# Low-rank layers on transposed activations: SP asks for all four x tiles of a group before the adapters, and asks for the A and B halves of the adapters separately

## What is computed

```
# layer 1: 8 adapters of rank 16, all in one 128-row matrix; ids per sequence
x = x + x @ W1.T + bias1 + scale[id] * (x @ A1[id].T) @ B1[id].T
# layer 2: 32 adapters of rank 16, gathered per sequence
x = x + x @ W2.T + bias2 + 2 * (x @ A2[id]) @ B2[id]
```

## Time and profile before

| | |
|---|---|
| median of 3 runs | 2545.6 us (2545.35 to 2546.51) |
| profiled execution, its own time | 2544.21 us |
| its span | 2542.6 us |
| PE busy over the span | 2409.0 us (95%) |
| changed stage, 105 to 317 us: PE busy | 162.41 of 212 us |
| granted PE clock in that stage | 0.88 of full speed (0.976 over the whole span) |

### The profile page before, as it was taken

The page is one execution under the profiler, slowest core; times in us unless marked ns, Lnnn a source line. Parts: engine busy times, 40 slices in busy tenths (PEclk is TensorE's granted clock), DMA queues, the critical chain, the costliest instruction groups (busy, mean ns, idle before and its releaser), DMA issues. The chain is left out here.

```text
span 2542.6 us, 54643 instructions
## 1 busy us (share of the span) xinstructions
PE 2409.0 (95%) x16070; PEld 2195.2 (86%) x16071; DVE 1780.3 (70%) x3632; ACT 1602.2 (63%) x3311; POOL 599.9 (24%) x896
## 2 busy tenths in 40 slices
PE   6878799999999979999999999999999997699999
PEld 4656688888888869999999999999999997588887
DVE  5434334989998977888878878788788884544443
ACT  3223235877777778888888888888888884311111
POOL 1200012000000024444444444444544442000000
PEclk9889999999999989999999999999999999799999
DMA  6521132333333469888888898888888884766664
GB/s 221 174 64 55 61 140 88 103 100 113 99 100 99 133 192 302 291 295 297 303 281 304 285 294 303 282 300 293 292 301 281 299 276 161 273 206 213 210 213 148
DMA packets 373752, 536.83 MB, mean 211 GB/s; under 512 B 49314, under 2 KB 263010, under 8 KB 369826
## 3 DMA queue, kind: packets, MB, share of 16 engines
q1 hardware_dynamic: 301538, 311.62, 38.2%
q0 software_dynamic: 70016, 221.30, 25.6%
q10 hardware_dynamic: 2112, 2.89, 0.4%
HBM read 437.35 MB, written 98.30 MB: 211 GB/s over the span
## 5 line engine op out<-in xcount | busy, mean ns | idle before, releaser
L1669 PE MATMUL both_ps_o<-att_pt,att_v 128*128 128x128 f32 x4096 | 539.3, 275 | 0.0
L1367 ACT ACTIVATE att_prob<-att_prob,att_shift 128x544 f32<-128x544 f32 x512 | 384.4, 751 | 205.5 <-DVE att_shift L1387 195.8
L1669 PEld LDWEIGHTS both_ps_o<-att_pt,att_v 128*128 128x128 f32 x4096 | 504.0, 191 | 0.0
L1387 DVE CUSTOM_DVE_ANT_0 att_prob<-both_ps_s,att_mask 128x544 f32<-128x544 f32 x512 | 365.0, 713 | 0.0
L102 PE MATMUL both_ps_s<-att_k_hi,att_q_hi 128*128 128x272 f32 x1024 | 339.2, 331 | 4.8 <-DVE att_k_lo L1362 4.8
L1362 DVE TENSOR_TENSOR att_k_lo<-att_k_raw,att_k_hi 128x1024 fp32r<-128x1024 f32 (+1 forms) x320 | 338.6, 1058 | 1.9 <-ACT att_k_hi L1356 1.9
L1646 PE MATMUL both_ps_pt<-both_ident,att_prob 128*128 128x128 f32 x2048 | 309.2, 274 | 7.8 <-ACT att_prob L1367 6.2
L104 PE MATMUL both_ps_s<-att_k_hi,att_q_lo 128*128 128x272 f32 x1024 | 298.0, 291 | 0.0
L1545 ACT ACTIVATE att_pt<-both_ps_pt 128x512 f32<-128x512 f32 x512 | 294.3, 575 | 2.2 <-PE both_ps_s L1654 1.2
L103 PE MATMUL both_ps_s<-att_k_lo,att_q_hi 128*128 128x272 f32 x1024 | 295.3, 288 | 0.0
L1356 ACT ACTIVATE att_k_hi<-att_k_raw 128x1024 fp32r<-128x1024 f32 (+1 forms) x320 | 292.7, 915 | 0.0
(11 more groups left out here) (209 smaller groups left out, 5036.0 us busy)
## 6 DMA issues: line engine op xcount, KB each, us to landing
att_k_raw<-in_k_pages SPq DMA_DIRECT2D x1024, 128.0 KB, 4.8
q_t<-qkv_out_t SPq DMA_DIRECT2D x128, 256.0 KB, 2.3
att_q_raw<-q_t POOLq DMA_DIRECT2D x64, 512.0 KB, 7.5
o_t<-att_o POOLq DMA_DIRECT2D x64, 512.0 KB, 7.0
out_o<-o_t SPq DMA_DIRECT2D x32, 1024.0 KB, 6.0
out_inv<-inv_t SPq DMA_DIRECT2D x32, 1024.0 KB, 6.6
both_w_stage<-in_w_qkv SPq DMA_DIRECT2D x12, 1024.0 KB, 5.2
l_w_stage<-in_w SPq DMA_DIRECT2D x8, 1024.0 KB, 7.4
```

The costliest lines, as they stand in the source:

```text
L1367: act.activation(prob[:, b, :], prob[:, b, :], ACT.Exp, bias=shift[:, b:b + 1], scale=-1.0, accum_out=total[:, j // HK, j % HK:j % HK + 1] ...
L1387: dve.tensor_tensor_reduce(out=prob[:, b, :].rearrange("p (a n) -> p a n", a=2), in0=ps_s[:, j % 2, :, 0:HALF], in1=mask[:, j // HK, :].re ...
L1669: pe.matmul(out, v_sb[p][:, c, h * DH:(h + 1) * DH], pt_sb[:, j % OG, c, :], start=(c == 0), stop=False)
```

## The change

SP's program in `lora_layers` is written in another order. All four x tiles of a group are asked for together; input tiles rotate through all four `x_sb` buffers (so x14 and x15, whose buffers the results z0 to z3 use as well, wait for the stores of those). In `load_adapters` the 8 A's of a half are issued in a row, as soon as the same half of the A buffer has been split, then the 8 B's, as soon as the same half of the B buffer has been split. Two semaphores (`a_loaded`, `b_loaded`), each counting both halves, replace one per half. No arithmetic changes, nor do the orders of PE and DVE.

```diff
                 def load_x(t):
                     if t >= 4:
-                        sp.wait_ge(turned, TURN_OF["x", t - 4 if t < 6 else t - 2] + 1)
-                    sp.dma_start(x_sb[:, x_buf(t), :], x_in[rows(t), :]).then_inc(x_loaded[x_buf(t)], 16)
+                        sp.wait_ge(turned, TURN_OF["x", t - 4] + 1)
+                    if t >= NT - 2:
+                        sp.wait_ge(both.x_stored[t % 2], 16 * 2)
+                    sp.dma_start(x_sb[:, t % 4, :], x_in[rows(t), :]).then_inc(x_loaded[t % 4], 16)
...
                         if g:
-                            sp.wait_ge(ab_split, 4 * g)
+                            sp.wait_ge(ab_split, 4 * (g - 1) + h + 1)
                         elif h:
                             sp.wait_ge(weights_split, FIRST_OF[W2])
                         for s, a in enumerate(adapters):
                             sp.dma_start(a_in[:, h, s * KC * RANK:(s + 1) * KC * RANK], i["a2"][bass.ds(a, 1)])\
-                              .then_inc(ab_loaded[h], 16)
+                              .then_inc(a_loaded, 16)
+                        if g:
+                            sp.wait_ge(ab_split, 4 * (g - 1) + 2 + h + 1)
+                        for s, a in enumerate(adapters):
                             sp.dma_start(b_in[s * RANK:(s + 1) * RANK, h, :], i["b2"][bass.ds(a, 1)])\
-                              .then_inc(ab_loaded[h], 16)
+                              .then_inc(b_loaded, 16)
...
-                for t in range(TPG, TPG + 2):
+                for t in range(TPG, 2 * TPG):
                     load_x(t)
                 sp.dma_start(w_in[:, 1, :, :], i["w2"]).then_inc(weights_loaded[W2], 16)
                 sp.wait_ge(ids2_loaded, 16)
                 load_adapters(0)
-                for t in range(TPG + 2, TPG + 4):
+                for t in range(2 * TPG, 3 * TPG):
                     load_x(t)
                 sp.wait_ge(weights_split, FIRST_OF[B1])
                 sp.dma_start(w_in[:, 0, :, :], w_next).then_inc(kept.w_loaded[0], 16)
-                for g in range(1, LG):
-                    if g < LG - 1:
-                        for t in range(TPG * (g + 1), TPG * (g + 1) + 2):
-                            load_x(t)
-                    load_adapters(g)
-                    if g < LG - 1:
-                        for t in range(TPG * (g + 1) + 2, TPG * (g + 2)):
-                            load_x(t)
-                    for t in range(TPG * (g - 1), TPG * g):
-                        store(t)
+                load_adapters(1)
+                for t in range(3 * TPG, NT - 2):
+                    load_x(t)
+                for t in range(TPG):
+                    store(t)
+                for t in range(NT - 2, NT):
+                    load_x(t)
+                load_adapters(2)
+                for t in range(TPG, 2 * TPG):
+                    store(t)
+                load_adapters(3)
+                for t in range(2 * TPG, NT - TPG):
+                    store(t)
...
                 def a_hi_part(g):
+                    act.wait_ge(a_loaded, 16 * 2 * HS * (g + 1))
+                    if g:
+                        act.wait_ge(low_done, ROUND_OF[1, g - 1] + 1)
                     for h in range(2):
-                        act.wait_ge(ab_loaded[h], 16 * 2 * HS * (g + 1))
-                        if g:
-                            act.wait_ge(low_done, ROUND_OF[1, g - 1] + 1)
...
                 def b_hi_part(g):
+                    act.wait_ge(b_loaded, 16 * 2 * HS * (g + 1))
```

More of the change, by code:

```diff
@@ L505, in lora_layers @@
         x_hi_done, x_split, z_copied = m.sem("x_hi_done"), m.sem("x_split"), m.sem("z_copied")
-        ab_loaded, ab_hi_done, ab_split = m.sems("ab_loaded", 2), m.sem("ab_hi_done"), m.sem("ab_split")
+        a_loaded, b_loaded, ab_hi_done, ab_split = m.sem("a_loaded"), m.sem("b_loaded"), m.sem("ab_hi_done"), m.sem("ab_split")
         low_done, masked = m.sem("low_done"), m.sem("masked")
@@ L525, in pieces @@
             return [(w_in[:, l, k, :], w_hi[:, l, k, :], w_lo[:, l, k, :]) for k in range(KC)]
[L527 to L531, removed]
         def tokens(g):
@@ L792, in transpose @@
                     if kind == "x":
-                        pe.wait_ge(x_loaded[x_buf(t)], 16 * x_loads(t))
+                        pe.wait_ge(x_loaded[t % 4], 16 * (t // 4 + 1))
                     else:
@@ L796, in transpose @@
                     for k in range(KC):
-                        src = x_sb[:, x_buf(t), k * P:(k + 1) * P] if kind == "x" else state[t // TPG % 3][:, k, in_group(t)]
+                        src = x_sb[:, t % 4, k * P:(k + 1) * P] if kind == "x" else state[t // TPG % 3][:, k, in_group(t)]
                         last = pe.transpose(ps_t[:, turn % 2, k, :], src, ident[:, :])
```

## The result

The changed kernel takes 2502.3 us (median of 4 runs, 2500.2 to 2504.5), the kernel before, beside it, 2546.1 (2545.4 to 2548.9). The ratio is 0.9826, 95% interval 0.9809 to 0.9843: 44 us faster, where 43.6 was forecast. That the medians agree to a few tenths is in part luck: the four runs spread over 4 us, the two profiled executions differ by 40.2 us, and in them the changed stage gained 41.65 us. One term of the sum was 1.4 us too large; the later stages did not make up for it.

The account below looks back on a forecast made before the run. PE was taken to stall on input tiles and A's issued late by SP, then run at the lower clock. 8.1 + 13.8 + 13.6 + 8.1 = 43.6 us off 2544.2, plus 1.4 to the median: 2502.0 us, range 2498 to 2510.5.

Parts of the forecast that it names:

- Rounds 2 and 4: Tiles x8 to x15 arrive before their turn, each round takes 18.7 us: 13.8 and 13.6 us go.
- Rounds 6 and 7: Group 3's adapters are issued sooner, so the chain from the last A to z8 comes 8.1 us earlier.
- the two branches at the end: Round 7, before z9: PE at full clock waits for `low_lo`, or at the lower clock arrives later without waiting.
- Round 0: x6 and x7 are in before PE wants them, so round 1 starts at 136.3 instead of 144.40: 8.1 us.
- The slack numbers: How early adapters' A's arrive before ACT asks: 9 us for group 1, 7 us for group 2.
- the slower rival's formula: SP issue time bounds (2%): d us over 0.52 per issue costs groups 3, 2, 1 24d, 24d - 7, 16d - 9.
- the stores queued behind the adapters: Stores z4 to z7 behind group 2's 32 issues: those end before z4 is copied in round 5, so no cost.
- The advice weighed there: The ramp's penalty isn't worth fitting; by that, summing brackets alone gives 36.0 us and 2509.6; the rows give 7.6 more.
- the clock's share: 7.6 us of the gain beyond the brackets; rival: PE loses it at the lower clock elsewhere, 2509.6 us, 3%.
- the chain of group 3: Rival: group 3's adapters come no earlier in effect, held by stores and B0's wait: 2510.1 us, 8%.
- its stall: Rival: round 7's stall goes altogether, the waits for z8 and `low_lo` vanish: 2 to 4 us more, 2499, 7%.
- no later stage gave anything back: Rival: a later stage, such as attention, gives the gain back: time near 2545 us, 5%.

Follow-up runs that it names:

- the tiles' part alone: The changed kernel with the adapters issued and waited for as before, only the input tiles asked for early: 2509.6 us, ratio 0.9855.
- Three kernels: Changed kernel with both halves' A's first (2499.4 us), with A's waiting for all four parts (2508.3), with extra issues behind group 3's adapters only (ratio 0.9908).
- the adapters alone: The kernel before with the changed kernel's rows of 8 A's and 8 B's and their waits, input tiles untouched: 2528.5 us, ratio 0.9924.
- the filled waits: The kernel before with unused matmuls on PE while it waits for x6, x10 and x14, no load earlier: 2541.7 us, ratio 0.9986.
- slowing the issues: The changed kernel with one more small DMA issued by SP behind each of the 128 adapter issues: 2547.0 us, ratio 1.0004.
- both A halves first: The changed kernel with both halves' A's issued in front of both halves' B's: 2499.4 us, ratio 0.9813; on another chip 0.9817.
- the filled kernel: The kernel with both halves' A's first plus 14, 5 and 8 unused transposes on PE at the stage's start: 0.981 of the kernel before.

## Why the prediction was right

*Rounds 2 and 4* (13.8 and 13.6): right to 0.1 us, and shown by the tiles' part alone, which keeps them at 18.65 and 18.64.

*Rounds 6 and 7* (8.1; 7.9 measured): the chain SP's last A, ACT, DVE's adds, z8 held in all places. The A parts began at T5 + 32.0 (242.61 - 210.60; 31.7 forecast), z8 at T5 + 40.9 (40.5). Three kernels moved ACT's A parts against T5 by -3.7, +4.6 (246.05 - 209.48) and +16.3 us (259.73 - 211.40); z9 in the first and z8 in the others moved by -4.0, +4.5 and +16.3. Of the two branches at the end, PE took the slow one: it worked at the lower clock and did not wait for `low_lo`.

*Round 0* (8.1; 6.7 measured) is the term that was mis-sized. The step that failed is "round 1 could start at 136.3": I took 8 us for the two stalled chunks and left the round's first part as it was in the trace before. But how long PE stays at the lower clock behind x0's wait differs from execution to execution. The first two rows are the kernel before, the last two the changed one: round 0's start and its first turned tile, x4.

```profile
116.24 0.79 PE L102 MATMUL lora_ps_low<-both_xt_hi,lora_a_hi 128*128 128x512 f32 x1 [1.90 <-DVE both_xt_lo L703]
120.43 0.60 PE L798 MATMUL lora_ps_t<-both_ident,lora_x 128*128 128x128 f32 x4
```

```profile
116.48 0.80 PE L102 MATMUL lora_ps_low<-both_xt_hi,lora_a_hi 128*128 128x512 f32 x1 [1.90 <-DVE both_xt_lo L706]
121.77 0.98 PE L801 MATMUL lora_ps_t<-both_ident,lora_x 128*128 128x128 f32 x4
```

The low-rank product takes 4.19 us there and 5.29 here, and x4's transposes 0.60 and 0.98. The change isn't the cause: it doesn't reach so far, and two variants of the kernel before (the adapters alone, the filled waits) take 5.29 and 5.28 as well. Round 0 without the wait for x6 took 21.42 (changed), 20.35, 21.30, 20.51 and 19.94 us in five kernels that feed it alike, and 20.37 to 21.43 in four later ones; the forecast's 20.06 lies in their range, near its lower end, and 18.6 is what it takes at full clock. w2, moved to 114.98, cost nothing: ACT starts on its hi parts at 128.56 with no idle time ahead of them.

*The slack numbers* for groups 1 and 2 were tested by slowing the issues. With d = 0.73 the slower rival's formula gives 64 x 0.73 - 16 = 30.7 us; measured were 44.6. So its crossing, at d = 0.93, was wrong: 0.73 is enough. It left out two things. Group 0's 32 issues were slowed as well, so group 1's first A went out at 158.58 instead of 143.84, and rounds 2 and 3 lost 10.3 us where the formula has 2.7. And the stores queued behind the adapters, which the prediction had called hidden, were not in the sum: rounds 6 and 7 up to z9, behind them, lost 22.9 us where it has 17.5. Rounds 4 and 5 lost 11.0, where it has 10.5.

*The advice weighed there*, the Trainium skill's "TensorE: Matmul & The Clock Gate", Part 1, that the ramp is below 1% of a span: so it is here, the forecast's 7.6 us of 2544 being 0.3%. But brackets alone would have given 36.0 us, and the filled waits, the stage's 41.65 us and the terms above side with the rows: the brackets that went come to 35.8 us, so the clock's share was 5.8.

*The other rivals* didn't happen: the chain of group 3 did come earlier, its stall didn't go altogether (that took both A halves first), most of the clock's share came back (5.8 of 7.6 us; the granted clock is 0.94 from 105 to 275.4 us, instead of 0.88), and no later stage gave anything back that stands out of its spread of 4 us.

The kernel with both A halves first is the fastest here, 0.9813 and 0.9817 of the kernel before on two chips; its 4 us over the changed kernel are seen in the trace, while the intervals of the ratios overlap.

## What to carry to other kernels

When one queue issues everything in program order, list for each transfer the earliest moment its buffer is free and the moment it is wanted, and look at what stands in front of it: here 32 small issues of 0.5 us each, not bandwidth, made 256 KB tiles 12 us late. Price a removed wait by the length of the whole round against a fed one, not by its bracket: the clock's share was 1.5 to 2.6 us per wait. And where an order leaves slack, count the stores behind it too, and what each row of issues does to the next: when the issues were slowed, late A's and late stores both reached PE.

## What the runs showed of the hardware

The clock can fall after the wait that caused it. In the changed kernel PE waits 2.47 us for z8, then turns it at full clock (251.54, 0.63 us for four) and starts its first matmul so; from the second on (252.24) they last 0.60 to 0.63 instead of 0.39, until 255.6. With both A halves first, without that wait, they last 0.39 to 0.40 there. In the kernel before, after longer waits, the tile's own transposes are slow already.

A small DMA between two places in device memory, issued by SP between others, cost 0.73 us of SP's time on the mean and not its own 0.49: its neighbours' issues lengthened from 0.38 to 0.52, and single ones took longer, one such copy 2.18 us. What in the queue does that was not tested.

One chip took 2636 us for the kernel before instead of 2546, with this stage unchanged (in the filled kernel the stage ends at 268.82 us, and the rest takes 2314.6 us of the span instead of some 2225). The extra time lies where the DMA engines are busiest: from 700 to 1800 us behind the stage PE makes some 805 matmuls in 100 us there, instead of 870 in the kernel with both A halves first, at the same granted clock of 1.00, while the DMA share is 0.82 instead of 0.88. What slows that chip's transfers, if it is they, isn't shown.
